# Attention output turned by VectorE in 32x32 blocks, and one ring of six PSUM banks, in a four-layer residual kernel

## The reference, cut to what matters

```python
x = x + _L0_cond_ref(x, ...)   # two small projections, rank 64
x = x + _L1_cond_ref(x, ...)   # rmsnorm, attention, Wo, rmsnorm, SwiGLU of width 1024
x = x + _L2_cond_ref(x, ...)   # attention; see below
x = x + _L3_cond_ref(x, ...)   # masked attention, Wo, rmsnorm, scale and shift

# _attention, 16 heads of 16 features
attn = jnp.einsum('blhd,bmhd->bhlm', q, k) / scale
p = jax.nn.softmax(attn, axis=-1)
o = jnp.einsum('bhlm,bmhd->blhd', p, v).reshape(B, L, D)
return o @ Wo.T

# _L2_cond_ref, between softmax and output
coh = jax.nn.sigmoid(jnp.tanh(comb @ Wc1.T + bc1) @ Wc2.T + bc2).transpose(0, 2, 1)
mod = attn * coh[..., None]
mod = mod / (mod.sum(-1, keepdims=True) + 1e-08)
fa = jax.nn.softmax(jnp.einsum('be,se->bs', fp, pe), axis=-1)     # one share per batch and token
mod = (1.0 - fi) * mod + fi * fa[:, None, :, None]                # fi = 0.21
out = jnp.einsum('bhij,bhjd->bhid', mod, v).transpose(0, 2, 1, 3).reshape(Bb, Ss, Ee)
return out @ Wout.T + bout
```

## Time and profile before

| | us |
|---|---|
| median of 3 runs (lowest, highest) | 1620.76 (1619.31, 1621.13) |
| profiled execution: its own time | 1620.15 |
| its span, from the first to the last instruction | 1618.4 |

### The profile page before, as it was taken

The page is one execution under the profiler, slowest core; times in us unless marked ns, Lnnn a source line. Parts: engine busy times, 40 slices in busy tenths (PEclk is TensorE's granted clock), DMA queues, the critical chain, the costliest instruction groups (busy, mean ns, idle before and its releaser), DMA issues. The chain is left out here.

```text
span 1618.4 us, 30453 instructions
## 1 busy us (share of the span) xinstructions
PE 1526.2 (94%) x10828; PEld 1277.4 (79%) x10828; DVE 1077.7 (67%) x3631; ACT 770.4 (48%) x1684; POOL 182.2 (11%) x219
## 2 busy tenths in 40 slices
PE   2579999999999999999999999999999999999997
PEld 1367888888888888888888888888877878787785
DVE  7756665555555665556657777777777777777774
ACT  1325444444444444444335555555555555555554
POOL 7400000000000000000000000000001011110102
PEclk9779999999999999999999999999999999999999
DMA  7074223233323222232135454454453444544340
GB/s 267 7 88 72 47 38 46 38 47 47 47 47 46 38 38 42 41 60 41 29 65 73 64 66 69 63 71 62 64 77 58 78 74 68 86 65 84 68 74 21
DMA packets 101120, 100.08 MB, mean 62 GB/s; under 512 B 11478, under 2 KB 97624, under 8 KB 100330
## 3 DMA queue, kind: packets, MB, share of 16 engines
q1 hardware_dynamic: 100970, 98.14, 37.3%
HBM read 16.83 MB, written 4.19 MB: 13 GB/s over the span
## 5 line engine op out<-in xcount | busy, mean ns | idle before, releaser
L920 ACT ACTIVATE work<-bank 128x512 f32<-128x512 f32 x768 | 448.6, 599 | 219.7 <-PE bank L1107 180.3
L527 DVE TENSOR_REDUCE rowmax<-bank 128x2 f32<-128x512 f32 x512 | 342.0, 687 | 147.8 <-PE bank L1097 144.6
L1107 PE MATMUL bank<-qs,ks 98*128 98x256 f32 x1536 | 405.8, 347 | 1.6 <-ACT work L920 0.8
L1097 PE MATMUL bank<-ks,qs 96*128 96x256 f32 x1536 | 350.9, 311 | 20.0 <-DVE rowmax L524 12.4
L1107 PEld LDWEIGHTS bank<-qs,ks 98*128 98x128 f32 x1536 | 271.8, 193 | 41.6 <-issue 17.7
L1097 PEld LDWEIGHTS bank<-ks,qs 96*128 96x128 f32 x1536 | 245.8, 191 | 50.9 <-DVE rowmax L524 16.7
L524 DVE CUSTOM_DVE_ANT_0 c1t<-bank,big_q 128x256 bf16<-128x256 f32 x512 | 190.3, 421 | 1.1 <-issue 0.3
L1119 PE MATMUL bank<-work,vp 128*32 128x256 f32 x3072 | 186.4, 383 | 0.0
L946 ACT ACTIVATE work<-bank 128x256 f32<-128x256 f32 x128 | 49.1, 383 | 201.9 <-PE bank L1166 201.9
L1119 PEld LDWEIGHTS bank<-work,vp 128*32 128x32 f32 x3072 | 90.1, 110 | 66.7 <-issue 6.9
L1166 PE MATMUL bank<-yt,w_gate 128*128 128x256 f32 x512 | 131.9, 379 | 2.1 <-ACT yt L940 2.1
(11 more groups left out here) (206 smaller groups left out, 1870.2 us busy)
## 6 DMA issues: line engine op xcount, KB each, us to landing
qs<-qk_hi SPq DMA_DIRECT2D x192, 128.0 KB, 3.9
ks<-qk_hi SPq DMA_DIRECT2D x192, 128.0 KB, 4.3
qs<-qk_lo SPq DMA_DIRECT2D x96, 128.0 KB, 4.4
ks<-qk_lo SPq DMA_DIRECT2D x96, 128.0 KB, 4.4
xres<-in_x_t SPq DMA_DIRECT2D x4, 1024.0 KB, 9.1
x_in<-in_x SPq DMA_DIRECT2D x16, 256.0 KB, 5.6
out<-xres SPq DMA_DIRECT2D x16, 256.0 KB, 2.1
qs<-nm SPq DMA_DIRECT2D x96, 16.0 KB
```

What stands on the lines that cost most here:

```text
L527: a = dve.tensor_reduce(rowmax[:, :, k:k + 1], bank[:, :].rearrange("p (t s) -> p t s", t=TC), AX, ALU.max)
L920: act.activation(probs[:, place[n, b, k], :, :], bank[:, :].rearrange("p (c s) -> p c s", c=TC), ACT.Exp, scale=HD ** -0.5)\
L1097: m = pe.matmul(bank[:, t * S:(t + 1) * S], qs[par][0:SCORE_ROWS, k, t * P:(t + 1) * P], ks[par][0:SCORE_ROWS, k, :], start=True, stop=True)
L1107: m = pe.matmul(bank[:, c * S:(c + 1) * S], ks[par][0:SHIFTED_ROWS, k, c * P:(c + 1) * P], qs[par][0:SHIFTED_ROWS, k, :], start=(n != 3), ...
```

## The change

- Both uses of TensorE's transposes for the attention output go. The `pv` bank is no longer copied by ScalarE but turned by VectorE in 32x32 blocks into `ot_raw`, once for each two groups; the sums are inverted (`rz`) and the output scaled (`norm`) from SBUF, in two halves; `oT` becomes two VectorE transposes of 128x256 in 32x32 blocks from `on` to `ot`. In this layout a token stands at (partition within a quadrant, block), and a quadrant of partitions holds four heads.
- Layer 2 follows that layout. The gate comes from two wider matmuls (`w_c2q`), ScalarE's exp takes the bias, and one VectorE transpose makes `coh`; the gate's formula is folded into one operation with the sum and one reciprocal (`COH_BASE`, `COH_SHIFT`). `sumv` is four matmuls of 32 rows in a ring bank, copied by ScalarE; GpSimd multiplies it by the shares (`field`), and adds it to `on` in its `norm` step.
- Layer 2's bias of v and output bias go from VectorE to GpSimd; ScalarE takes v and the output projection from PSUM. Layer 3's factor `some_key` goes from VectorE's `rz` to GpSimd's inverse root.
- The two rings become one of six banks.
- `SLOT` and `LATER` have other values for many steps, with new steps `rz` and `norm` and none called `tok` or `spread`. `sumv` goes from slot 19.68 to 4.0 and `wo` of layer 2 from 25.09 to 22.05. The load of the weights of layer 2's output projection hangs on SyncE's `wo` step instead of `field`.

```diff
+TB = S // HW
 SLOT = {
     1: {
-        "smax": -13.9, "pv": (8.35, 15.57), ... "v": -11.72, "tok": 18.52, ... "oT": 20.77, "wo": 22.0, ...
+        "smax": -13.9, "pv": (8.3, 16.3), "rz": (8.59, 16.41), "norm": (8.44, 16.81), ... "oT": 18.5, "wo": 21.54, ...
     2: {
-        "smax": -14.7, "pv": (9.43, 16.53), ... "tok": 18.5, ... "sumv": 19.68, "field": 20.62, "oT": 22.3, "wo": 25.09},
+        "smax": -14.72, "pv": (9.43, 17.26), "rz": (9.93, 17.56), "norm": (14.07, 17.86), ... "sumv": 4.0, "field": 5.0, "oT": 19.5, "wo": 22.05},
     3: {
-        "smax": -14.01, "pv": (9.2, 15.39), ... "tok": 18.48, "mod": 13.22, "oT": 20.92, "wo": 22.34, "squares": 22.35, "resid": 24.21},
+        "smax": -13.86, "pv": (9.2, 15.39), "rz": (9.7, 15.69), "norm": (10.2, 15.99), ... "mod": 14.15, "oT": 16.94, "wo": 20.71, "squares": 23.07, "resid": 24.6},
...
-        head = Ring(sem("head_full"), banks[0:2])
-        middle = back = Ring(sem("scores_full"), banks[2:6])
+        head = middle = back = Ring(sem("banks_full"), banks[0:6])
...
@@ vector
                 if what == "shares":
...
+                    for w in range(QUADS):
+                        dve.transpose(field[HW * w:HW * (w + 1), :, :].rearrange("p j w -> p (j w)"), fld[:, 0, :]).then_inc(s_field, 1)
...
-                    if what == "v" and n == 2:
...
                     if what == "coh3":
                         dve.wait_ge(ez_ok.sem, ez_ok.at(b, 1))
-                        ...three operations on [128, 32]
+                        dve.transpose(coh[par][:, :, :].rearrange("p j w -> p (j w)"), ez).then_inc(coh_ok.sem, 1)
-                    if what == "tok":
...
-                    if what == "field":
...
+                    if what == "pv" and k % 2 == 1:
+                        u = k // 2
+                        dve.wait_ge(L.pv.sem, L.pv.at(b, k + 1))
+                        dve.transpose(ot_raw[:, DC * u:DC * (u + 1), :].rearrange("p c s -> p (c s)"), pv_bank[:, :]).then_inc(L.o_raw.sem, 1)
+                    if what == "rz":
+                        dve.wait_ge(L.o_raw.sem, L.o_raw.at(b, k + 1))
+                        total = turned_o[:, k, :, :, HD]
                         if n == 2:
+                            dve.wait_ge(coh_ok.sem, coh_ok.at(b, 1))
+                            dve.scalar_tensor_tensor(rz[:, k, :, :], coh[par][...], COH_BASE, total, ALU.add, ALU.mult).then_inc(rz_coh.sem, 1)
...
+                        dve.reciprocal(rz[:, k, :, :], total).then_inc(L.rz.sem, 1)
+                    if what == "norm":
+                        dve.wait_ge(L.rz.sem, L.rz.at(b, k + 1))
...
+                        dve.tensor_tensor(on[:, :, :, k, :]..., turned_o[:, k, :, :, 0:HD]..., rz[:, k, :, :]...to_broadcast([P, DC * TB, HD]), ALU.mult)\
+                            .then_inc(L.on.sem, 1)
+                    if what == "oT":
...
+                        dve.wait_ge(L.wo.sem, L.wo.at(b, 0))
+                        for c in range(DC):
+                            dve.transpose(ot[:, c, :], on[:, c, :, :, :].rearrange("p j u d -> p (j u d)")).then_inc(L.ot.sem, 1)
-                    if what == "wo" and n == 2:
...
@@ sync
-                    if what == "field" and n == 2 and b == 0:
+                    if what == "wo" and n == 2 and b == 0:
                         sp.wait_ge(hm_ok.sem, hm_ok.at(NBATCH, 0))
@@ gpsimd
+                    if what == "v" and n == 2:
+                        pool.wait_ge(v_raw.sem, v_raw.at(b, 1))
+                        pool.tensor_tensor(vp[par][:, :, :, 0:HD], vp[par][:, :, :, 0:HD], bv_rows..., ALU.add).then_inc(L.vp.sem, 1)
                     if what == "vsum":
+                        pool.tensor_tensor(xres[:, b, :, :], xres[:, b, :, :], bout_rows..., ALU.add).then_inc(bias_ok.sem, 1)
...
+                    if what == "field":
...
+                        for c in range(DC):
+                            a = pool.tensor_tensor(field_v[:, c, :, :], share_v[:, c, :]..., field[:, :, b:b + 1]..., ALU.mult)
+                    if what == "norm" and n == 2 and k == DC - 1:
...
+                        pool.tensor_tensor(flat, flat, x_in[:, :, :].rearrange("p t d -> p (t d)"), ALU.add).then_inc(on_field.sem, 1)
@@ scalar
-                    if what == "pv" and k % 2 == 1:
...
-                    if what == "oT":
...
+                    if what == "wo" and n == 2:
...
+                        act.copy(y[:], acc_bank[:, :].rearrange("p (t d) -> p t d", t=TC)).then_inc(attn2_ok.sem, 1)
@@ tensor
                     if what == "coh2":
-                        tokens_first(bank, c1t, w_c2, width=H).then_inc(head.sem, 1)
+                        for i in range(DC):
+                            m = pe.matmul(bank[:, 0:S], w_c2q[:, i, :, :].rearrange("p q w -> p (q w)"), c1t[:, i, :], start=(i == 0), stop=(i == DC - 1))
                     if what == "sumv":
-                        pe.matmul(acc_bank[:, 0:D], ones[:], vsum, start=True, stop=True).then_inc(sumv_ok.sem, 1)
-                    if what == "tok":
...
-                                m = pe.transpose(bank[:, g * P:(g + 1) * P], ot_raw[:, g, t * P:(t + 1) * P], ident[:])
-                    if what == "oT":
...
-                        transposes(bank, on).then_inc(head.sem, 1)
+                        bank = head.wait_free(pe, n, b, "sumv")
+                        for quad in range(QUADS):
+                            m = pe.matmul(bank[HW * quad:HW * (quad + 1), 0:DC * HW], ones[:, 0:HW], vsum...[:, quad, :, :], start=True, stop=True)
```

More of the change, by code:

```diff
@@ L1 @@
+import math
 from contextlib import ExitStack
@@ L55 @@
-ONCE = {"ortho": -33.5, "top": -30.3, "shares": -26.5, "spread": -22.0}
+        "smax": -13.9, "pv": (8.3, 16.3), "rz": (8.59, 16.41), "norm": (8.44, 16.81), "neg": (-6.41, 1.59),
+        "max": (-6.11, 4.35), "xT": -26.99, "q": -24.35, "stack": (-25.3, -22.08, -15.9, -16.88), "k": -22.83, "v": -12.2,
+        "load": -46, "rank": -32.95, "cond": -30.74, "squares": -30.51, "xn": -28.27, "oT": 18.5, "wo": 21.54, "yn": 23.31,
+        "yT": 24.38, "ffn": (25.73, 1.15), "down": (27.4, 1.24)},
+    2: {
+        "smax": -14.72, "pv": (9.43, 17.26), "rz": (9.93, 17.56), "norm": (14.07, 17.86), "neg": (-6.46, 1.15),
+        "max": (-6.52, 2.71), "xT": -26.47, "q": -24.49, "stack": (-23.72, -22.05, -15.9, -15.63), "k": -24.09, "v": -11.32,
+        "load": -30, "coh1": -13.18, "coh2": -10.81, "coh3": -10.31, "vsum": 1.0, "sumv": 4.0, "field": 5.0, "oT": 19.5,
+        "wo": 22.05},
@@ L237, in cond_resid_kernel @@
         vp = [sb(f"vp{i}", [P, TC, H, HW]) for i in range(2)]
-        coh = [sb(f"coh{i}", [P, TC, H]) for i in range(2)]
+        coh = [sb(f"coh{i}", [P, TB, HW]) for i in range(2)]
         x_in, c1t = sb("x_in", [P, TC, D]), sb("c1t", [P, DC, S])
@@ L900, in step @@
                         a.then_inc(L.qk_hi.sem, 1)
-                    if what == "v" and n != 2:
+                    if what == "v":
                         bank = head.wait_filled(act, n, b, "v")
-                        act.copy(vp[par][:, :, :, 0:HD], bank[:, :].rearrange("p (t h d) -> p t h d", t=TC, h=H)).then_inc(L.vp.sem, 1)
+                        done = v_raw if n == 2 else L.vp
+                        act.copy(vp[par][:, :, :, 0:HD], bank[:, :].rearrange("p (t h d) -> p t h d", t=TC, h=H)).then_inc(done.sem, 1)
                     if what == "coh1":
                         bank = head.wait_filled(act, n, b, "coh1")
+                        act.wait_ge(coh_ok.sem, coh_ok.at(b, 0))
                         for c in range(DC):
@@ L909, in step @@
                     if what == "coh2":
-                        act.wait_ge(zz_ok.sem, zz_ok.at(b, 1))
-                        act.wait_ge(coh_ok.sem, coh_ok.at(b, 0))
-                        act.activation(ez[:], zz[:], ACT.Exp, scale=-1.0).then_inc(ez_ok.sem, 1)
+                        bank = head.wait_filled(act, n, b, "coh2")
+                        if b == 0:
+                            act.wait_ge(s_coh, 4 + DC + QUADS)
+                        act.activation(ez, bank[:, 0:S], ACT.Exp, scale=-1.0, bias=bc2_q[:, 0:1]).then_inc(ez_ok.sem, 1)
+                    if what == "sumv":
+                        bank = head.wait_filled(act, n, b, "sumv")
+                        act.wait_ge(field_ok.sem, field_ok.at(b, 0))
+                        act.copy(share_v, bank[:, 0:DC * HW].rearrange("p (c w) -> p c w", c=DC)).then_inc(share_ok.sem, 1)
                     if what == "probs":
@@ L1017, in once @@
                     pe.matmul(banks[4][0:C, 0:1], sgn[:], ones[0:C, 0:1], start=True, stop=True).then_inc(s_sign, 1)
-                if what == "shares":
-                    pe.wait_ge(s_shares, 1)
-                    for t in range(TC):
-                        m = pe.transpose(banks[7][:, t * NBATCH:(t + 1) * NBATCH], fld[:, 1, t * P:(t + 1) * P], ident[0:NBATCH, 0:NBATCH])
-                    m.then_inc(s_fa, 1)
             def steps_of(n):
```

212 lines of the change are left out of this document (113 added, 99 removed), and 5 rows, old and new, of the table SLOT.

## The result

The changed kernel takes 1537.45 us (median of 4 runs, 1535.91 to 1538.69), the one before 1620.74 beside it: a ratio of 0.9487, 95% interval 0.9471 to 0.9504, 83 us less.

What follows compares the result with a forecast made beforehand. TensorE's instruction stream was taken as the bound: 1620.15 us less 59.0 for transposes and 2 for the tail gave 1559, with the other terms at zero. The range was 1541 to 1586 us.

Steps and rivals of the forecast that it cites:

- the ring: Six shared score banks in layer 3, idle time in layers 1 and 3: 18 us gained to 12 lost, taken as zero.
- the ring gives the idle time back as well: Rival: TensorE's idle time waiting for banks is recovered too, 18 us more, giving 1541 us; chance 0.10.
- tail: Last batch, from the attention output's turn to the output projection: 2.1 us after instead of 4.3, gain 2 us.
- Transposes leaving TensorE: TensorE, all layers: 1.23 us a batch less from start to start, 59.0 us in 48 batches; modelled ends gave 1.64.
- `coh2` and `sumv`: TensorE in layer 2: the reshaped matmuls of both steps, taken together as zero change.
- The pessimistic end: TensorE in layer 2: small matmuls into separate quadrants don't overlap, +1.6 us a batch, 26 us.
- VectorE's account: VectorE's work a batch goes to 27.9, 18.0 and 20.8 us, 66%, 77% and 89% full; TensorE stays the bound.
- The rival of 200 ns for 32 columns: VectorE's wide transposes cost 200 ns per 32 columns, +64 us, giving 1684 us; chance 0.05.
- Its rival: VectorE becomes the bound in layer 3, which keeps 24.7 us a batch; layer 2 gets half; 1588 us; chance 0.13.
- GpSimd and the port: Layer 2: GpSimd's added work delays VectorE by 0.9 us a batch, covered by slack; taken as nothing, uncovered 14 us.
- Moved waits: Steps around the pv bank, `oT`, `wo` and GpSimd's addition in `norm`: TensorE does not wait, taken as nothing.
- load of the weights: SyncE's load for layer 2's `wo`: margin falls from 6.5 to 1.9 us; nothing, once 3 us at worst.

## Why the prediction was wrong

**The term that failed is the ring.** I read rows 4 as 0.73 us a batch to be had in layer 3, weighed it against a fuller VectorE, and took zero between 18 us gained and 12 lost. Alone, merging gives 19 us (0.06, 0.48 and 0.65 a batch), and in the changed kernel the split costs 41. My upper end of 18 us rested on recorded idle time, and so missed layer 2, where the waits were inside "busy" matmuls; and VectorE's load did not cancel the gain, as I had weighed it. The rival that came nearest, "the ring gives the idle time back as well" at 1541, had a chance of 0.10, and what I held against it was that load. Why the ring is worth 41 us now and 19 before is argued and not shown: VectorE is fuller, but the times of the steps are others too, and some 8 of the 41 us are the clock, by the estimate above.

With that, the sum closes: transposes 61 us, ring 19, tail 2, which is 82 of the 83. That it closes so well is partly luck, for what is left differs by layer and cancels. From the merged ring's period less the transposes' price, layer 1 should be at 43.73 - 1.29 = 42.44 and is at 41.85; layer 3 at 22.84 and is at 22.51; layer 2 at 22.73 and is at 23.61. Layer 1's 0.6 includes 0.38 of `h_rank` wait, which the new times took away; I had kept it. What the other 0.2 and layer 3's 0.33 are was not isolated. Of layer 2's loss of 0.9, 0.64 comes back when both its limits are lifted; the rest is open.

**A second term had no line in my sum: the new times of the steps.** I priced only the waits that single moves might bring, and so put the rest at nothing. In the changed kernel the old times cost 78 us. With them layer 1 stands at 43.19 us, 0.75 above the 42.44 to be expected, so the new layout by itself lost something that its new times gave back. The times' own share of the 83 us can't be told from these runs, since they were never tried on the kernel before.

**Transposes leaving TensorE:** right. 1.23 us a batch from start to start, against 1.25 to 1.39 measured; the 1.64 of the modelled ends would have been too much.

**`coh2` and `sumv`:** taken as zero together, and near it. From start to start `coh2` is now 0.68 us for 0.81 (1018.12 to 1018.93 before), and `sumv`, eight records of 64 columns, 0.25 (the next matmul starts at 1001.50) for 0.24 (1013.12 to 1013.36 before). The pessimistic end, small matmuls that don't overlap, is out.

```profile
1001.25 0.32 PE L1168 MATMUL bank<-xn,ones 128*32 128x64 f32 x8
...
1003.81 1.03 PE L1132 MATMUL bank<-c1t,w_c2q 128*128 128x256 f32 x4
1004.49 0.59 PE L1139 MATMUL bank<-ks,qs 96*128 96x256 f32 x2
```

**VectorE's account:** right in its prices (0.69 and 0.42 us for the wide transposes, measured 0.70 and 0.42; 89% forecast in layer 3, 87% measured). In us a batch, layer 3 came to 225.96/260 x 22.51 = 19.6, not 20.8. Some 0.5 of the difference is in the two operations that make `negs`, of which one was slow beside GpSimd (below); the rest was not isolated. The rival of 200 ns for 32 columns is out, and the Trainium skill's sentence in "Vector Engine (DVE) Microarchitecture Reference", section 3.8, holds on this trace: 128x512 takes as long as the reduction of the same size. What I drew from the account was incomplete: full to 89% on average is no bound only as long as a buffer covers the bursts. Its rival very nearly came true when the ring was split.

**GpSimd and the port:** taken as nothing, and the two additions tested cost nothing. A `norm` took 711 ns once beside GpSimd instead of 424; in the Trainium skill's terms ("SBUF — State Buffer", "Who interferes with whom") that is the lock. For `norm` it is rare, one time in 96. In layer 3 it is not: one of the two operations that make `negs`, the one with a single input (L534), takes 166 ns at the least and 654 at the median of 23 from 1240 to 1500 us, beside GpSimd's two additions. In the kernel before it was the other, with 176 at the median and 1218 at the most. The new times have moved the meeting, and VectorE has some 0.5 us a batch less to do (both operations together 20.8 us in 310 before, 13.7 in 260 after). VectorE does stand for GpSimd's `norm` addition (10.1 us in the 13 batches from 870 to 1190 us, 0.8 us each, forecast half a microsecond).

**Moved waits, load of the weights, tail:** right. TensorE never waits for the weights. The tail, in the last batch of the changed kernel:

```profile
1521.71 0.72 DVE L545 STREAM_TRANSPOSE ot_raw<-bank 128x512 f32<-128x512 f32 x1 [0.65 <-PE bank L1161]
...
1523.79 1.97 PE L1185 MATMUL bank<-w_hid,ot 128*128 128x256 f32 x8 [2.15 <-DVE ot L570]
```

2.08 us from turn to output projection, for 4.3 in the earlier trace rows and a forecast of 2.1.

**Not foreseen at all** was the DMA path of layer 2. The stacks and the maxima go through one queue, and with the new times both orders of the two have a price. The clock was not foreseen either: it stays at 1.00 in layer 2 of the changed kernel, and falls in several of the runs that wait more there.

## What to carry to other kernels

Read an engine's pace, not only its idle time: where the same instruction starts every 0.34 us in one place and every 0.24 in another, the difference is a wait that "busy" hides. When work moves from the bounding engine to one that then runs near 90%, price the buffer between them as part of the move; six shared banks instead of two and four were worth 19 us before the move and 41 after it, with new times in between. When waits grow, look at the granted clock as well: it can cost as much as the waits. And when a stage gains less than its parts add up to, lift the suspected limits together as well as alone: here `rz` and `oT` later gave nothing alone and 5 us once the DMAs were small.

## What the runs showed of the hardware

A VectorE transpose in 32x32 blocks costs no more than another operation over the same columns: 702 ns for 128x512 float32 from PSUM, 418 ns for 128x256 in SBUF, 200 ns for 32x32. Four matmuls of 64 columns into four quadrants of one bank, with 32 columns of weights each, take about a quarter of a microsecond from start to start, in eight records. Where TensorE waited for a DMA of 16 KB that stood behind transfers of 128 KB on the same queue, its matmul started some 5.1 us after the last of these had been issued (medians of 5.0 to 5.2 in six runs of 11 to 13 such waits), with two transfers ahead as with three. After three waits of 0.3 to 0.9 us within 3 us the granted clock fell (0.72 on average over 905 to 911 us), and 32 matmuls took 3.42 us instead of 1.93.
